# The first norm's centring and square begun two tiles sooner in a fused attention and expert kernel

## The reference, cut to what matters

```
h = h + attention(layernorm(h))      # first norm; 64-wide Q, K, V; 1024 x 1024 scores
h = h + ffn(layernorm(h))            # second norm; 8 experts, gated by the mean over batches

layernorm(x) = (x - mean(x)) / sqrt(var(x) + 1e-5)
M       = where(W == 0, 0, tril)     # W are the scores
x_exp   = exp(W - max(W)) * M        # the max is over the whole row, the future included
A       = x_exp / (sum(x_exp) + 1e-9)
```

## Time and profile before

| what | value |
|---|---|
| median of 3 runs | 381.75 us |
| profiled execution, own time | 379.69 us |
| its span, first to last instruction | 377.7 us |
| PE busy | 351.0 us, 93% |
| DVE busy | 265.7 us, 70% |
| ACT busy | 208.2 us, 55% |
| POOL busy | 130.2 us, 34% |
| mean granted clock of TensorE | 0.995 |

### The profile page before, as it was taken

One profiled execution on the slowest core, in us unless ns is written; L12 is line 12 of the kernel. 1 busy time (PEld: TensorE's weight loads), 2 busy tenths in 40 slices (PEclk: granted clock), 3 DMA queues, 4 the chain that ended last, 5 costly groups with the idle time before them and its releaser, 6 DMA issues.

```text
span 377.7 us, 8006 instructions
## 1 busy us (share of the span) xinstructions
PE 351.0 (93%) x2690; PEld 168.1 (45%) x2690; DVE 265.7 (70%) x576; ACT 208.2 (55%) x435; POOL 130.2 (34%) x202
## 2 busy tenths in 40 slices
PE   4889999999989989989989989997999999999985
PEld 2655344356346346435545535444554333333321
DVE  3223858789879879879888888988635566566673
ACT  0133655568457557557558568578564545664500
POOL 7060302435345354453453654435506500000000
PEclk9999999999999999999999999999989999999999
DMA  6999741904603801900000000000000011110112
GB/s 147 223 218 193 144 91 42 183 0 97 130 0 71 153 0 48 174 0 0 0 2 3 2 0 2 1 2 0 3 0 3 2 30 28 30 29 1 30 29 57
DMA packets 28992, 20.45 MB, mean 54 GB/s; under 512 B 12280, under 2 KB 28832, under 8 KB 28960
## 3 DMA queue, kind: packets, MB, share of 16 engines
q1 hardware_dynamic: 28352, 19.91, 26.3%
q10 hardware_dynamic: 608, 0.12, 0.2%
HBM read 17.93 MB, written 2.10 MB: 53 GB/s over the span
## 4 chain that ended last, share of the span: by engine, by line
PE 70%; DVE 11%; issue 7%; ACT 7%; POOL 2%; DMA 1%; DVEq 0%; SPq 0%; ACTq 0%; POOLq 0%
PE Sp L1368 10%; PE Sp L1636 7%; PE MM L1679 6%; PE PTp L1657 6%; PE MM L1302 5%; PE PTp L1380 4%; PE MM L1423 4%; PE MM L1299 3%; DVE SN L910 3%; PE MM L1431 2%; PE MM L1276 2%; PE MM L1280 2%; DVE EP L910 2%; ACT EP L631 2%; ACT PT L566 2%
## 5 line engine op out<-in xcount | busy, mean ns | idle before, releaser
L1368 PE MATMUL Sp<-eT,G 64*64 64x512 f32 x512 | 69.6, 603 | 0.9 <-ACT E2T L566 0.9
L424 POOL TENSOR_SCALAR_AFFINE_SELECT EP<-EP 128x128 f32<-128x128 f32 x64 | 23.6, 368 | 116.7 <-ACT EP L628 108.8
L566 ACT ACTIVATE PT<-PTp 128x512 f32<-128x512 f32 (+2 forms) x96 | 42.7, 487 | 23.5 <-PE PTp L1380 19.2
L910 DVE TENSOR_SCALAR_CACHE_REDUCE EP<-Sp,sr 128x1024 f32<-128x1024 f32 x32 | 40.3, 1274 | 2.0 <-PE Sp L1368 2.0
L910 DVE TENSOR_SCALAR_CACHE_REDUCE SN<-Sp,sr 128x1024 f32<-128x1024 f32 x32 | 40.2, 1279 | 1.3 <-PE Sp L1368 1.2
L1368 PEld LDWEIGHTS Sp<-eT,G 64*64 64x64 f32 x512 | 19.2, 132 | 29.7 <-issue 29.5
L1423 PE MATMUL MM<-PT,e 128*64 128x512 f32 (+3 forms) x176 | 31.4, 489 | 0.1
L919 DVE SCALAR_TENSOR_TENSOR SN<-SN,EP 128x384 f32<-128x384 f32 (+3 forms) x32 | 29.4, 918 | 1.6 <-POOL EP L424 1.2
L1636 PE MATMUL Sp<-E2T,W1f 64*64 64x512 f32 x232 | 29.5, 615 | 0.3 <-ACT h L789 0.3
L919 DVE SCALAR_TENSOR_TENSOR EP<-EP 128x128 f32<-128x128 f32 (+3 forms) x32 | 22.6, 705 | 8.7 <-POOL EP L424 7.7
L1197 DVE SCALAR_TENSOR_TENSOR PT<-PTp,negc,XW 128x512 f32<-128x512 f32 x28 | 19.7, 744 | 12.1 <-PE PTp L1657 11.5
(11 more groups left out here) (312 smaller groups left out, 693.6 us busy)
## 6 DMA issues: line engine op xcount, KB each, us to landing
XW<-in_x_dram SPq DMA_DIRECT2D x6, 1024.0 KB, 11.3
X<-in_x_dram SPq DMA_DIRECT2D x6, 1024.0 KB, 9.7
out_dram<-xc SPq DMA_DIRECT2D x8, 256.0 KB, 2.6
XW<-in_x_dram SPq DMA_DIRECT2D x2, 576.0 KB, 8.6
X<-in_x_dram SPq DMA_DIRECT2D x2, 576.0 KB, 13.9
XW<-in_x_dram SPq DMA_DIRECT2D x2, 448.0 KB, 11.4
X<-in_x_dram SPq DMA_DIRECT2D x2, 448.0 KB, 13.3
EP<-in_L_tok_W_dram SPq DMA_DIRECT2D x2, 144.0 KB, 3.3
```

The source lines that it names most:

```text
L424: pool.affine_select(out=blk_, in_=blk_, compare_op=ALU.is_ge, fill=0.0, base=0, pattern=[[-1, 128]], channel_multiplier=1).then_inc(tri_d ...
L566: return act.activation(dst, src, ACT.Copy)
L910: dve.tensor_scalar(W4[t % 4], Sp[t % 2][:, :], -SCALE, sr[q][:, place(t), 0:1], ALU.mult, ALU.min, accum_out=negm[q][:, t:t + 1]).then_in ...
L1368: ins = pe.matmul(Sp[t % 2][64 * s:64 * s + 64, CH * c:CH * c + CH], G[q][rows, 128 * t + 64 * s:128 * t + 64 * s + 64], eT[q][rows, :], **ON)
```

## The change

The centring of the norm of batch b+2 is now issued in `pairs(b)`, between the masks of tile 0 and tile 1 of batch b+1, instead of at the start of `pairs(b+1)`. The square follows at the end of `pairs(b)` on ACT. The sum of squares and POOL's power then stand first in `pairs(b+1)`. On ACT the exponential of tile 1 moves ahead of the copy of E2T, and `class_exp` goes behind `et_copy` and the exponential of tile 5. On DVE `p0_rest` goes ahead of the mask of tile 3. The pieces that stand at the seams (behind batch 0 and in batch 6) are moved to match. No instruction is added or removed in all, apart from register work. PE's and SP's programs are the same.

```diff
 POOL
             def pairs(b):
+                ln1_rstd(b + 1)
                 tri(b, 2)
                 tri(b, 3)
-                ln1_rstd(b + 1)
...
                     if t == 0 and after_pairs:
-                        pass
+                        ln1_rstd(b + 1)
 ACT
                 pt_copy(b, 1)
-                ln1_sq(b + 1, 1 - q)
                 expo(b, q, 2)
...
                 expo(b, q, 4)
-                class_exp(b, 0)
                 et_copy(b + 1, 1 - q, Sp[0])
                 expo(b, q, 5)
+                class_exp(b, 0)
...
                 pt_copy(b, 7)
+                expo(b + 1, 1 - q, 1)
                 e2t_copy(b - 1, Sp[0])
-                expo(b + 1, 1 - q, 1)
+                ln1_sq(b + 2, q)
 DVE
                 class_arg(b - 1, 1 - q, 1)
-                ln1_centre(b + 1)
+                ln1_ss(b + 1, 1 - q)
                 smax(b, q, 2)
                 smax(b, q, 3)
                 mask(b, q, 2)
-                ln1_ss(b + 1, 1 - q)
+                p0_rest(b - 1, 1 - q, 1)
                 mask(b, q, 3)
-                p0_rest(b - 1, 1 - q, 1)
...
                 mask(b + 1, 1 - q, 0)
+                ln1_centre(b + 2)
                 mask(b + 1, 1 - q, 1)
...
                     if not last:
-                        if t == late:
+                        if t == late and not after_pairs:
                             ln1_centre(b + 1)
-                        if t == 1 + late:
+                        if t == (0 if after_pairs else 1 + late):
                             ln1_ss(b + 1, 1 - q)
```

More of the change, by code:

```diff
@@ L504, in body @@
                     if not last:
-                        if t == 1 + late:
+                        if t == 1 + late and not after_pairs:
                             ln1_rstd(b + 1)
@@ L755, in body @@
                         h_copy(1)
-                    if t == late and not last:
+                    if t == late and not last and not after_pairs:
                         ln1_sq(b + 1, 1 - q)
@@ L798, in _ @@
             expo(1, 1, 1)
+            ln1_sq(2, 0)
             with act.Fori(0, NB // 2 - 2) as j:
@@ L1103, in _ @@
             mask(1, 1, 0)
+            ln1_centre(2)
             mask(1, 1, 1)
```

## The result

The changed kernel takes 375.13 us, the median of five runs, against 381.07 us, the median of five of the kernel before on the same chip. The ratio is 0.9852, with a 95% interval of 0.9823 to 0.9881, or 5.6 us; it leaves out the one execution of the changed kernel that fell in a slower state (379.81 us). A second set of six runs gave 374.61 and a ratio of 0.9844 (0.9797 to 0.9890). The direction and the mechanism were as forecast, the size was 5.6 instead of 4.85, and 375.13 lies 0.7 under the stated range.

The account below looks back on a forecast made before the run. The ring of DVE and POOL (29.4 us a batch against PE's 28.07) was taken as the bound. Batches 2 to 4 save 3.99, batch 5 1.16, less 0.2: 4.95 us, giving 376.8, stated as 376.9; range 375.8 to 379.7.

Parts of the forecast that it names:

- the ring of DVE and POOL: DVE and POOL waiting on each other in batches by twos; claimed period 29.4 us, above PE's own 28.07, so setting the pace.
- the remaining 0.15: Part of the 1.31 us a held batch loses, beyond 1.16 at L1338; guessed to be `et_copy` standing behind `class_exp` on ACT.
- The ring's new period: DVE and POOL after the change, per batch: 29.38 - 1.28 - 1.33 + 0.2 + 0.1 = 27.1 us, under PE's 28.07.
- the lock: POOL's addition and `feat_sum` holding up DVE's centring and mask 1 through the shared port pair; charged 0.2 us of delay.
- my worst case: Centring's second step waits for POOL's addition, its third for `feat_sum`: centring ends at 127.3, mask 1 at 127.6, against 126.0.
- the page's rule: Skill page: DVE instructions with two SBUF inputs contend with GpSimd ones reading SBUF, reductions never; two of three centring steps exposed.
- rival 1: DVE and POOL again the bound through port contention: period 28.7, gain 2.6 us, 379.2 us; chance 0.15.
- the later copy of E2T: ACT's copy behind the exponential at each batch's end: delayed 0.69 us to 125.0, with 0.4 of cover before PE overwrites the bank.
- The mis-sized term: batch 5: Batch 5 wins the 1.16 us wait at L1338, less 0.2 at its end for the delayed copy of E2T.
- the listed wait for UT: PE's wait of 0.51 us ahead of `o_group` of batch 6; claimed to give back 0.5 of the copy's 0.69 delay.
- the 1.16: Loss at L1338, where turning normed tokens began 2.00 us after `o_group` instead of 0.84; counted as batch 5's gain.
- Rival 3: Copy of E2T comes late behind the exponential of tile 1 and stops PE: four batches lose 3.2 us, 385.0; chance 0.06.

Follow-up runs that it names:

- `pure_centre`: Kernel before with only the centring and the square moved; sum of squares, power and both ScalarE exchanges as before: batches 2 to 4 mean 28.34 us, 29.40 before.

## Why the prediction was right and where it was wrong

*The bound: right.* That the ring of DVE and POOL set 29.4 and PE's own work 28 is shown from both sides: 0.6 of filling costs 0.6 before and nothing after, in batches 2 to 4. The guess for the remaining 0.15 was right too, and it was 0.22: `g_quarters` begins 2.52 after `e_turn_early` in those batches and 2.30 in the changed kernel.

*The ring's new period: right in sum (27.0 for 27.1), not in its parts.* I charged the lock with 0.2. The rows show a centring and a mask of 3.6 us from 121.96 to 125.6 where 1.9 are work, so 1.7 lost, nearly my worst case; 1.06 came back at `class_arg`, which I had left at 1.21. The net loss to the lock was thus 0.6 and not 0.2; what made up for the difference no run here separates. The 0.2 rested on a misreading: the earlier trace rows do not show a whole centring beside `feat_sum`. That `feat_sum` ends at 215.28, L885 ends with it, at 215.31, and the third step starts only behind it:

```profile
215.35 0.69 DVE L887 TENSOR_TENSOR xc<-H,st 128x512 f32<-128x512 f32 x1
```

So the page's rule was the better guide here, and one sign of rival 1 came, L888 over a microsecond. Its windows of 28.5 did not, since the lock is mostly moved: what the centring and mask 1 lose, `class_arg` no longer does.

*Batches 1 to 4.* Forecast 0 + 1.31 + 1.37 + 1.31 = 3.99; measured 0.09 + 1.12 + 1.46 + 1.39 = 4.06. Two errors met. PE's own work is 27.98, not 28.07: batch 1 of before held a small wait of its own, at L1348. And batch 2 pays 0.28 for the later copy of E2T at the loop's turn, which I had said was covered.

*The mis-sized term: batch 5.* Forecast 1.16 - 0.2 = 0.96; measured 0.73 at batch 6's `score` and 0.69 more up to its `o_group`, 1.42. The copy cost 0.57. But I let at most 0.5 come back for PE, by the listed wait for UT; by starts the stretch had 0.69 to give, so the end of the batch gained 0.12 where I charged 0.2. That gain needs the early centring and the early power both (6.52 and 6.11 without one of them, 6.20 before). And the 1.16 was batch 2's wait: in batch 5 `e_turn_early` came 2.12 after `o_group`, 1.28 late, and L1348 gave 0.03 more. Sum 5.48 against 4.95, which I then rounded down to 4.85.

*The range: too tight below.* 375.8 was 381.75 less 5.95, which I called 5.3 of PE's waits and a little of DVE's; the listed waits are 4.2 and 0.9 and 0.5 for UT, 5.6 in all. But 381.75 was a median of three runs of a kernel whose spans run from 376.3 to 380.5 at mean clocks of 0.995 to 0.987, and five runs of it gave 381.07. I had carried the bounds of my terms into the range and nothing for that spread. The 0.68 between the two medians is all of the 0.67 by which the time lies under the range: against 381.07 the saving of medians is 5.94, at the very end of what I had allowed, 5.95. Had batch 5 not been mis-sized, the range would have been half a microsecond wider below as well.

*What the small steps were worth.* `class_exp` costs something only while DVE is late: in `pure_centre`, with the old order, `g_quarters` begins 2.46, 2.52 and 2.53 after `e_turn_early` in batches 2 to 4, against 2.30, which is about half of what its 28.34 lie above 27.98; putting the old order back in the changed kernel cost nothing. In the length of batches 2 to 4 ScalarE's two exchanges are worth 0.66 alone (29.40 - 28.74), the centring 1.06 alone (29.40 - 28.34), both 1.4, and the power shortens the ring by another 1.0; PE cuts the sum of 2.4 off after 1.4. I had counted the last as necessary for batches 2 to 4, and it was not; what it gave was 0.6 to 0.8, once, in batch 6.

None of the rivals came about. Rival 3's place was the right one to watch: it is where the changed kernel still loses 0.28 and 0.57.

## What to carry to other kernels

When two rings share a period, measure the spare time of the faster one with a known filling, not by adding up idle gaps: gaps that a change removes are cashed only until the next engine binds, here 1.4 of 2.4 us a batch. Then look at the seams for the rest: a filling that batches 2 to 4 absorbed cost 0.6 at batch 6. A step moved on a queue that the bound engine waits for costs most at the seams, where the cover of the steady state is missing. And a forecast in absolute time needs the spread of the baseline in its range, before any bound of its own terms.

## What the runs showed of the hardware

POOL's `feat_sum` of 1.45 us held a DVE instruction of 4 columns up for 1.06 us, and shrinking it to 8 columns gave each batch 1.0 us, with no semaphore between the two. The spells at TensorE's 1.2 GHz level fall differently from one execution to the next of one program: the granted mean was 0.977 to 0.995 for the changed kernel, its spans 371.1 to 377.7. What starts a spell these runs do not settle.
